# Two reorderings at the head of each iteration of a Mamba-and-attention decoder layer: the state products on TensorE, and four pieces of work on VectorE

## The reference

```python
proj = input_states @ in_proj_w.T                 # 512 -> 8192 gate, 8192 x, 1024 B, 1024 C, 128 dt
xBC = silu(conv4(xBC) + conv_b)                   # causal, 4 taps, per channel
...
scores = einsum('bcihn,bcjhn->bcijh', C, B) * Ldec * dt   # Ldec = masked exp(cum_i - cum_j)
y = scores @ x (+ state terms) + D * x
g = y * silu(gate)
g = g * rsqrt(mean(g*g over a group) + eps) * norm_w
x = x + g @ out_w.T
```

## Time and profile before

| what | value |
|---|---|
| median of 3 runs | 2847.14 us (2843.8 to 2848.58) |
| the profiled execution's own time | 2843.42 us |
| span of the core in it | 2841.6 us |
| mean granted TensorE clock | 0.997 |
| PE busy | 2804.8 us (99%) |
| DVE busy | 1990.1 us (70%) |
| ACT busy | 1462.6 us (51%) |
| POOL busy | 1315.5 us (46%) |

### The profile page before, as it was taken

How to read it: one execution, slowest core, us unless ns; L and a number is a source line. 1 busy time by engine, 2 the same in 40 slices (tenths; PEclk the granted TensorE clock), 3 DMA queues, 4 the chain that set the end, 5 groups by cost and what they waited for, 6 DMA issues and landing times.

```text
span 2841.6 us, 56494 instructions
## 1 busy us (share of the span) xinstructions
PE 2804.8 (99%) x22298; PEld 2274.4 (80%) x22298; DVE 1990.1 (70%) x3152; ACT 1462.6 (51%) x2205; POOL 1315.5 (46%) x840
## 2 busy tenths in 40 slices
PE   7999999999999999999999999999999999999998
PEld 5788888878788788887888888888888888878886
DVE  8777768887667757677676766677666666666767
ACT  5666656655445545445445454544545444453545
POOL 4766767775344333443343443424434334343334
PEclk9999999999999999999999999999999999999999
DMA  7788777778565555565665665555656656555530
GB/s 253 274 298 300 264 270 258 269 257 291 181 200 189 181 183 182 181 192 182 203 193 180 200 189 174 186 180 185 203 180 192 193 173 203 181 184 187 186 130 31
DMA packets 179428, 578.27 MB, mean 203 GB/s; under 512 B 25248, under 2 KB 31904, under 8 KB 171104
## 3 DMA queue, kind: packets, MB, share of 16 engines
q1 hardware_dynamic: 179168, 574.66, 61.5%
HBM read 460.29 MB, written 114.29 MB: 202 GB/s over the span
## 4 chain that ended last, share of the span: by engine, by line
PE 91%; DVE 6%; ACT 1%; issue 1%; DMA 0%; POOL 0%; SPq 0%; DVEq 0%; ACTq 0%; POOLq 0%
PE p_in L472 53%; PE p_out L472 23%; PE p_y L472 9%; PE p_in L562 4%; DVE cv L1430 1%; PE p_y L700 1%; DVE o_ring L1370 1%; DVE t_y L1479 0%; DVE g_f L1491 0%; DVE mx L1600 0%; ACT cv L942 0%; DVE sc L1587 0%; DVE cum L1392 0%; DMA raw_w<-wt 0%; DVE decay L1462 0%
## 5 line engine op out<-in xcount | busy, mean ns | idle before, releaser
L472 PE MATMUL p_in<-xnb,w_ring 128*128 128x512 f32 x6864 | 1673.2, 396 | 1.8 <-DVE cv L1430 0.9
L472 PEld LDWEIGHTS p_in<-xnb,w_ring 128*128 128x128 f32 x6864 | 1260.8, 188 | 262.6 <-issue 2.7
L1430 DVE SCALAR_TENSOR_TENSOR cv<-p_in,cpar,cv 128x504 f32<-128x504 f32 x954 | 699.8, 734 | 469.2 <-ACT cv L942 445.4
L1856 POOL TENSOR_TENSOR g_lo<-g_f,g_hi 128x512 fp32r<-128x512 f32 x256 | 338.1, 1322 | 1195.8 <-ACT g_hi L942 1195.8
L472 PE MATMUL p_out<-o_ring,g_hi 128*128 128x512 f32 x2048 | 638.3, 393 | 1.7 <-POOL g_lo L1856 1.7
L942 ACT ACTIVATE cv<-p_in,cpar 128x512 f32<-128x512 f32 x318 | 246.6, 775 | 636.9 <-PE p_in L472 600.5
L472 PEld LDWEIGHTS p_out<-o_ring,g_hi 128*128 128x128 f32 x2048 | 379.4, 188 | 80.3 <-issue 2.3
L472 PE MATMUL p_out<-o_ring,g_lo 128*128 128x512 f32 x1024 | 399.6, 390 | 0.0
L1467 DVE TENSOR_TENSOR x_tok<-p_in,dts 128x512 f32<-128x512 f32 x256 | 176.5, 689 | 285.7 <-PE p_in L562 284.0
L942 ACT ACTIVATE x_t<-cv 128x512 f32<-128x512 f32 x256 | 160.9, 628 | 309.9 <-DVE t_y L1479 285.9
L1867 POOL TENSOR_TENSOR ss<-ss,g_sq 128x512 f32<-128x512 f32 x190 | 310.3, 1633 | 7.4
(11 more groups left out here) (258 smaller groups left out, 2251.4 us busy)
## 6 DMA issues: line engine op xcount, KB each, us to landing
w_ring<-ws_scr SPq DMA_DIRECT2D x432, 512.0 KB, 3.7
o_ring<-ows_scr SPq DMA_DIRECT2D x192, 512.0 KB, 4.6
ws_scr<-w_ring SPq DMA_DIRECT2D x144, 512.0 KB, 5.9
decay<-cum_scr SPq DMA_DIRECT2D x126, 512.0 KB, 6.7
raw_w<-wt SPq DMA_DIRECT2D x144, 256.0 KB, 5.1
ows_scr<-o_ring SPq DMA_DIRECT2D x64, 512.0 KB, 6.3
raw_o<-owt SPq DMA_DIRECT2D x64, 256.5 KB, 5.6
acb<-x SPq DMA_DIRECT2D x3, 1024.0 KB, 7.7
```

The costliest lines, as they stand in the source:

```text
L472: return nc.tensor.matmul(o, lhsT=l, rhs=r, start=first, stop=last)
L1430: ins = V.scalar_tensor_tensor(acc[:, :, t:SEQ], src[:, :, 0:SEQ - t], cpar[:, 5 * m + 3 - t:5 * m + 4 - t], acc[:, :, t:SEQ], ALU.mult, A ...
L1856: T(g_lo[:, c % 2, :], g_f[:, c % 2, :], g_hi[:, c % 2, :].bitcast(F32), ALU.subtract).then_inc(glo_done, 1)
```

## The change

On TensorE, in the iterations behind the first, `project` of chunk 6 and `state_products` change places. On VectorE `late(0)` goes to the front of `products`, and `decayed(0)` goes behind `x_tokens(0)`. Nothing is added or left out, and nothing is moved on ScalarE, GpSimd or SyncE.

```diff
@@ tensor engine, body @@
                 unit(3, tb, g, n)
                 if begun:
+                    project(CPG - 2, *back)
                     state_products(n)
-                    project(CPG - 2, *back)
                     to_tokens(0, n)
 
                     unit(4, tb, g, n)
@@ vector engine, body @@
                 if not begun:
                     conv(3, n)
+                if begun:
+                    late(0, tb, g)
                 products(n)
                 if not begun:
                     dve.wait_ge(dtk_done, 2)
                     steps(tb, g)
-                else:
-                    dve.wait_ge(cbt_done, n + 1)
-                    decayed(0, n)
                 dve.wait_ge(dts_done, n + 1)
                 x_tokens(0, n)
                 if not begun:
                     clamped_half(0)
                 if begun:
-                    late(0, tb, g)
+                    dve.wait_ge(cbt_done, n + 1)
+                    decayed(0, n)
                     spread(0, tb, g)
                     refill_o(0)
```

## The result

The changed kernel takes **2877.28 us** (median of 4 runs, 2874.92 to 2891.31), the kernel before 2845.47 us in the same session (2841.96 to 2848.58). The ratio is 1.0122, interval 1.0087 to 1.0157: 31.8 us slower. The forecast was 2871, range 2857 to 2890. The profiled execution is the one of 2891.31 us, with a span of 2889.5, and is thus the longest of the four; what follows from its rows is set against its own span, 47.9 us above that of before.

The account below looks back on a forecast made before the run. TensorE's queue was taken as the bound (busy 2804.8 of 2841.6 us). Terms 10.5 (wait for g_lo) + 4.7 (even groups) + 8.4 (block 0) = 23.6 us on the median 2847.14 gave 2871 us, range 2857 to 2890.

Parts of the forecast that it names:

- The wait for g_lo: TensorE's output product of chunk 6, brought forward, waits for GpSimd's g_lo: 0.34 us in each of 31 iterations, 10.5 us.
- odd groups: Odd groups of blocks 1 to 3: the decay product fits between two GpSimd shifts; nothing beyond 0.34 us per iteration.
- The sign given for it: Output product's first matmul behind unit 3 names g_lo as releaser, with about 0.3 us of idle, 31 times.
- Even groups: Blocks 1 to 3, 12 iterations: decay product waits for GpSimd's 2048-column subtraction, making conv(3) and chunk 1's transposes late: 4.7 us.
- the lock's part: In even groups, VectorE and GpSimd instructions blocking each other: 0.36 us in each of 11 iterations, 0.7 in iteration 8.
- Block 0: Iterations 1 to 7, where GpSimd runs two weight splits: decay product first, stalls mostly in iterations 5 and 6, 8.4 us.
- a tie: Block 0: VectorE's decay product and GpSimd's second weight split start 0.03 us apart; priced with the decay product ahead.
- The prediction's own sign for that: Iterations 1 to 4 growing by more than 2 us each would show the decay product losing to the second split.
- The rival, GpSimd wins everywhere: Second weight split starts first throughout block 0, so decay product and o_low come late: 17 us more, 2888 us; chance 22%.
- the terms "3.7" and "4.2" of iterations 5 and 6: Lateness of chunk 1's transposes in us, with o_low waiting for the subtraction: 3.7 in iteration 5, 4.2 in 6.
- the 3.6 of the rival: Cost in us in each of iterations 1 to 4 if GpSimd's second split always goes first; chance 22%.

Follow-up runs that it names:

- Experiment 3: Changed kernel with ScalarE's rounding of chunk 6 (g_hi) moved ahead of its first tap of conv(2): 2877.23 us, ratio 1.0101.
- experiment 4: Changed kernel with GpSimd waiting for the decay product before block 0's second weight split and the subtraction in blocks 1 to 3: 2858.48 us, ratio 1.0042.
- the second execution: Changed kernel run again unaltered for another profiled execution: median 2880.25 us, ratio 1.0127, span of the profiled one 2885.3.
- kernel 6: Changed kernel with VectorE's decay product in block 0 held until GpSimd's first weight split is done: 2897.54 us, ratio 1.0181.
- experiment 5: Changed kernel with ScalarE's early chunk 6 rounding and GpSimd waiting for o_low (block 0) or the decay product (blocks 1 to 3): 2846.29 us, ratio 1.0002.

## Why the prediction was right, and where it was not

**The wait for g_lo: right.** 0.31 us in odd groups, where 0.34 was predicted, with the predicted 0.14 us from g_lo's end to the first matmul. Over 31 iterations 9.6 us for 10.5. The sign given for it, an idle of about 0.3 us, doesn't show as such: g_lo is the releaser 31 times, but with a recorded idle of 0.14 (0.23 in one place); the loss shows in the distance between starts. Experiment 3 shows that it hangs on ScalarE's rounding of chunk 6 and goes with it.

**Even groups: right.** 0.57 instead of 0.70 in all; the lock's part is 0.26 us instead of 0.36, and 0.9 in iteration 8: 3.7 us for 4.7. Half of that difference is a slip: conv(3) from 1581.62, 2.27, 0.62 and the hops of 0.05 and 0.14 add up to 1584.70, not 1584.75. The decay product was to take 4.6 us and took 4.68; the sums of squares were to fall from 4.60 to 2.67 and took 2.73. Experiments 3 and 4 each remove the extra, by different means.

**Block 0: the mechanism was right, the size wrong, in two of its steps.** The first is the one that reads "The second split would start at 452.06 + 3.90 + 1.25 = 457.21, and the decay product at 452.06 + 5.12 = 457.18: a tie", and goes on to price block 0 with the decay product ahead in every iteration. The tie was there, within the 0.03 us; giving it to VectorE throughout is what failed. The prediction's own sign for that, a growth of more than 2 us in iterations 1 to 4, came up in three, two and three of the four in the three traced executions. The rival, GpSimd wins everywhere, was put at 2888 us; forced, it takes 2897.5. What happens lies between: some ties are lost in each execution.

The second step is the terms "3.7" and "4.2" of iterations 5 and 6, and the 3.6 of the rival: they price a late chunk 1 at TensorE's stall alone. With the slow clock behind it, a lost tie in iterations 1 to 4 costs 5.2 to 6.4 us beyond the wait. Iterations 5 and 6 grew by 5.1 and 5.7 us beyond the wait in the second execution, where VectorE won both ties, against 3.7 and 4.2 in the sum.

**The sum again**, with what was measured: the wait 9.6, even groups 3.7, iterations 5 and 6 10.8, what is left of block 0 with every tie won 4 x 0.3 = 1.2 (nothing for iteration 7, an estimate, since no traced execution won its tie): 25.3 us. That this is about the 23.6 of the forecast is luck in part: its terms were a little high outside block 0 and too low in it. The median lies 31.8 above before; the 6.5 us in between are about the price of one lost tie among iterations 1 to 4. The first profiled execution adds up from its own rows: iterations 1 to 3 lost, 17.3 us beyond the wait, 4 won, 0.3, 5 and 6 12.6, 7 lost, 3.1; with 9.6 and 3.7 that is 46.6 of 47.9. The three traced executions of the changed kernel, at 2891.31, 2887.14 and 2891.84 us, lie 16 to 21 us above the forecast; only the untraced ones bring the median within 6 us of it. That the timed runs lose fewer ties than the profiled ones, whose times are the highest in both sets of the changed kernel, is inferred from the times (the profiled execution of kernel 6, with all ties lost in each, is the highest of its set too); no trace shows it, and why it would be so stays open.

**Who has the lock.** The page "SBUF — State Buffer" (the Trainium skill, section "SBUF: two separate sides") has the exclusive lock for a whole instruction. The traces here agree: 4.68 us for 2.28, 4.17 for 0.74, and the extra is gone where GpSimd waits for the instruction (2.28 us in experiment 4, 0.75 for o_low of chunk 0 in experiment 5). That the first starter has it holds down to some 20 ns here; nearer than that the recorded starts don't tell it: at -6 and -4 ns the decay product lost, at -3 it won twice and lost once.

## What to carry to other kernels

When a wait on an engine in front moves other instructions, list where VectorE's instructions with two SBUF inputs now start against GpSimd's, in every kind of iteration. A meeting costs the rest of the other's instruction, and whatever is queued behind the loser is late by a second one; here 0.74 us became 4.17. Where two starts are within some 30 ns of each other, price both outcomes and expect both in one run, or settle the order with a wait: letting GpSimd wait took some 23 us off. A stall of a few microseconds on TensorE has to be priced with the slow stretch behind it: here 1.4 to 1.8 us on stalls of 2.9 to 3.7 us.

## What the runs showed of the hardware that was not expected

- **A tie is settled anew each time.** The same program lost 5, 3 and 4 of 7 ties in three executions, with starts 2 to 34 ns apart; all starts of -23 ns or earlier won, all of +2 or later lost, and in between both came up.
- **TensorE's clock behind a stall.** Over the traces of all these kernels, behind the first 50 us, no stall of 0.9 to 1.7 us was followed by a slow stretch unless a longer one came between. Of 58 stalls of 2.4 to 4.5 us 49 were: behind 45 the 128x512 matmuls are 0.43 us apart instead of 0.23, and behind four, in iteration 7 of four traces, the granted clock was 0.50 too, but mostly narrower matmuls ran in it. The longest without one was 3.34 us, and all of 3.58 us or more had one.
- **Idle TensorE can cost more than useless work.** 98 extra matmuls (14 in each of 7 iterations) in the stalls of block 0 took 11 us off the kernel that always loses the tie.
